# Two-layer AdaLN/MoE kernel: the second layer's input and token rows turned by transposing DMAs instead of identity matmuls

## What is computed

```python
# layer 0: per-sequence mixed weight, then a top-2 mixture of 8 linear experts
h = einsum('bnt,bot->bno', x, einsum('bg,got->bot', cond, weight * mask)) + bias
probs = softmax(h @ router_w.T); top-2 of 8
x = x + sum over the two experts of (h @ expert_w + prob) * topk_weight
# layer 1: per-sequence projection with LoRA, then shared and routed SwiGLU
h = einsum('btc,oc->bto', x, W_base) + b_base + 2 * lora(x, As, Bs, cond)
shared = sum over 2 experts of silu(h @ wg) * (h @ wu) @ wd        # width 352 each
probs = softmax(h @ gate_w); top-2 of 8, weights normalized
routed = sum over the two experts of w * swiglu_e(h)
x = x + shared + routed
```

## Time and profile before

| | |
|---|---|
| median of 3 runs | 382.75 us (382.38 to 382.76) |
| the profiled execution | 382.96 us, its span 380.9 us |
| PE busy | 362.4 us, 95% of the span |
| DVE, ACT, POOL busy | 63%, 44%, 41% |
| granted TensorE clock, mean | 0.993 of full speed |

### The profile page before, as it was taken

How to read it: one execution, slowest core, us unless ns; L and a number is a source line. 1 busy time by engine, 2 the same in 40 slices (tenths; PEclk the granted TensorE clock), 3 DMA queues, 4 the chain that set the end, 5 groups by cost and what they waited for, 6 DMA issues and landing times.

```text
span 380.9 us, 7891 instructions
## 1 busy us (share of the span) xinstructions
PE 362.4 (95%) x2671; PEld 222.6 (58%) x2672; DVE 238.6 (63%) x594; ACT 166.6 (44%) x286; POOL 155.8 (41%) x241
## 2 busy tenths in 40 slices
PE   7998999999999999889999899999999999999992
PEld 2354444454454555455446677777777777766570
DVE  1367999776657547787774455565556556546574
ACT  1145377467655675451441333333333333322560
POOL 3000564656537631000020365565565556422652
PEclk9999999999999999999999999999999999999997
DMA  7975213433353410100000122222222222213922
GB/s 232 391 289 202 75 41 108 147 114 113 129 179 98 141 55 2 56 2 0 2 28 2 42 85 83 69 83 81 71 81 83 82 70 83 69 43 138 353 90 109
DMA packets 18037, 39.24 MB, mean 103 GB/s; under 512 B 2976, under 2 KB 9376, under 8 KB 17888
## 3 DMA queue, kind: packets, MB, share of 16 engines
q1 hardware_dynamic: 13552, 28.71, 22.2%
q0 software_dynamic: 3744, 10.23, 8.5%
q10 hardware_dynamic: 720, 0.02, 0.1%
HBM read 29.65 MB, written 9.31 MB: 102 GB/s over the span
## 4 chain that ended last, share of the span: by engine, by line
PE 73%; DVE 16%; issue 3%; ACT 3%; DMA 2%; POOL 1%; POOLq 0%; ACTq 0%; SPq 0%; DVEq 0%
PE bank L998 57%; PE bank L1145 7%; PE bank L1243 3%; DVE prod L903 2%; DVE x L776 2%; PE bank L1227 2%; PE bank L1014 2%; ACT acts L581 2%; DMA x<-wc 2%; DVE x L891 1%; DVE w0s L646 1%; DVE acts L908 1%; DVE hs L634 1%; ACT sil L571 1%; PE bank L1074 1%
## 5 line engine op out<-in xcount | busy, mean ns | idle before, releaser
L442 POOL TENSOR_TENSOR w1s<-piece,w1s 128x170 f16<-128x170 f32 x128 | 61.6, 520 | 78.5 <-ACT piece L531 78.5
L998 PE MATMUL bank<-w0s,hs 128*128 128x512 f16 x384 | 86.2, 379 | 1.4 <-DVE x L776 1.2
L998 PE MATMUL bank<-w1s,rT 128*128 x468 | 76.2, 313 | 1.5 <-DVE rT L962 1.5
L451 POOL DMA_INDIRECT rows<-token_store,row_in x39 | 38.0, 974 | 88.2 <-DVE row_in L873 48.5
L776 DVE SCALAR_TENSOR_TENSOR x<-bank,coef,x 128x256 f32<-128x256 f32 x128 | 54.8, 478 | 19.3 <-PE bank L998 19.0
L998 PEld LDWEIGHTS bank<-w0s,hs 128*128 128x128 f16 x384 | 36.9, 98 | 44.1 <-DVE x L776 1.9
L998 PE MATMUL bank<-hs,w1s 128*128 128x512 f16 x264 | 59.3, 379 | 1.9 <-DVE prod L903 1.9
L998 PEld LDWEIGHTS bank<-w1s,rT 128*128 128x128 f16 x468 | 44.0, 98 | 22.0 <-issue 2.0
L456 POOL DMA_INDIRECT results<-yb,row_out x39 | 38.6, 990 | 37.0 <-ACT yb L605 37.0
L998 PE MATMUL bank<-w1s,aT 128*128 (+1 forms) x351 | 44.8, 272 | 0.8 <-DVE aT L955 0.8
L599 ACT ACTIVATE ract<-prod 128x352 f16<-128x352 f32 x39 | 19.4, 498 | 58.4 <-DVE prod L968 33.6
(11 more groups left out here) (149 smaller groups left out, 405.4 us busy)
## 6 DMA issues: line engine op xcount, KB each, us to landing
piece<-w SPq DMA_DIRECT2D x16, 680.0 KB, 3.9
w1s<-results SPq DMA_DIRECT2D x6, 512.0 KB, 9.4
x<-wc SPq DMA_DIRECT2D x4, 512.0 KB, 6.7
w1s<-xT SPq DMA_DIRECT2D x4, 512.0 KB, 10.2
w1s<-w SPq DMA_DIRECT2D x4, 512.0 KB, 8.8
token_store<-xrow SPq DMA_DIRECT2D x4, 512.0 KB, 2.9
out<-x SPq DMA_DIRECT2D x8, 256.0 KB, 2.0
x<-x SPq DMA_DIRECT2D x1, 1536.0 KB, 10.6
```

Of the source, the lines that this page charges most:

```text
L442: ins = nc.gpsimd.tensor_tensor(w1s[:, LO, at], piece[:, i % 2, part], w1s[:, HI, at], ALU.subtract)
L451: pool.indirect_dma_start(rows[:, i % 2], None, token_store, bass.IndirectOffsetOnAxis(row_in[:, i:i + 1], 0)).then_inc(s_row[i % 2], 16)
L998: mm = nc.tensor.matmul(out_ap, l, r, start=(i == 0), stop=(i == len(terms) - 1))
```

## The change

The input of layer 1 is split into halves first, in the layout in which `x1` lies (`xh`, a new buffer of 256 KB for one pair of tiles), and then turned by one transposing DMA for each pair from SP, `turn_input(m)`. The token rows of a chunk are turned by four transposing DMAs, `turn_rows(c)`, from `hs` into `xrow`. PE's `transposes` and `token_rows`, and ACT's `copy_rows`, are gone. `tr_hi(m)` waits for the combines of its pair and, as `xh` is a single buffer, for the turn before. `tr_lo(m-1)` stands behind j=0 instead of j=2. On SP, turn_input stands behind pieces 3, 5, ... 15 and at the end, turn_rows behind pieces 8 and 12, keep behind pieces 9 and 13 (waiting for the transfers of turn_rows to land), and at the end come turn_rows(2), keep(2), turn_input(7), turn_rows(3), keep(3). layer1_input(3) and all of the routing move one step of gate_up later, down(0) too.

```diff
-    DOWN = {ST + 1: 0, EARLY - 1: 1, EARLY + 1: 2}
+    DOWN = {ST + 2: 0, EARLY - 1: 1, EARLY + 1: 2}
...
+        xh = sb("xh", [P, 2, 2, D], F16)
...
+            def turn_input(m):
+                sp.wait_ge(sm["s_trlo"], m + 1)
+                sp.dma_start_transpose(xrow[:, 2 * m:2 * m + 2].rearrange("p t (b n) -> p (t b) n", n=P),
+                                       xh[:].rearrange("p t a w -> p (t a w)")).then_inc(sm["s_xt"], 16)
+
+            def turn_rows(c):
+                sp.wait_ge(sm["s_hlo"], (B + c + 1) * KT)
+                for a in range(2):
+                    for k in range(KT):
+                        o = (a * KT + k) * P
+                        sp.dma_start_transpose(xrow[:, c * TPB:(c + 1) * TPB, o:o + P],
+                                               hs[:, a, k, c * S:(c + 1) * S]).then_inc(sm["s_rows"], 16)
+
             def keep(c):
-                sp.wait_ge(sm["s_rows"], (c + 1) * TPB)
+                sp.wait_ge(sm["s_rows"], 16 * 2 * KT * (c + 1))
...
                 sp.dma_start(piece[:, i % 2], w1_flat[:, i * PIECE:(i + 1) * PIECE]).then_inc(s_piece[i], 16)
+                if i >= 3 and i % 2 == 1:
+                    turn_input(i // 2 - 1)
                 if i in (8, 12):
+                    turn_rows(i // 4 - 2)
+                if i in (9, 13):
                     keep(i // 4 - 2)
 
+            turn_rows(2)
             keep(2)
+            turn_input(TWO - 1)
+            turn_rows(3)
             keep(3)
...
             def tr_hi(m):
-                act.wait_ge(sm["s_tr"], m + 1)
-                nc.scalar.activation(xs[:, 2 * m:2 * m + 2, HI], turned(), ACT.Copy, scale=SX).then_inc(sm["s_trhi"], 1)
+                act.wait_ge(sm["s_comb"], (m + 1) * 2 * E)
+                if m == 0:
+                    act.wait_ge(sm["s_bias"], 2)
+                else:
+                    act.wait_ge(sm["s_xt"], 16 * m)
+                nc.scalar.activation(xh[:, :, HI], x1[:, 2 * m:2 * m + 2], ACT.Copy, scale=SX).then_inc(sm["s_trhi"], 1)
...
-                if m >= 3 and m % 2 == 1:
-                    copy_rows((m - 3) // 2)
...
-                if i == 1:
+                if i == 2:
                     h_hi(1, B - 1)
...
-                    if j == 2 and m >= 1:
+                    if j == 0 and m >= 1:
                         tr_lo(m - 1)
...
-                if i == 2:
+                if i == 3:
                     take_logits(1, 0, ALL)
...
-                if i == 14:
+                if i == 15:
                     tile_experts()
...
             def layer1_input(c):
 
-                pe.wait_ge(sm["s_trlo"], (c + 1) * TPB // 2)
+                pe.wait_ge(sm["s_xt"], 16 * (c + 1) * TPB // 2)
                 pe.wait_ge(sm["s_wllo"], c + 1)
-                if c >= 1:
-                    pe.wait_ge(sm["s_rows"], c * TPB)
...
-                    if j == 1 and m >= 1:
-                        transposes(m - 1)
...
-                gate_up(i, TWO - 1 if i == 0 else None)
-                if i == 1:
+                gate_up(i)
+                if i == 2:
                     layer1_input(B - 1)
-                if i == 2:
+                if i == 3:
                     logits(1, B - 1)
-                if i == 3:
-                    token_rows(B - 1, (0, 1))
-                if i == 4:
-                    token_rows(B - 1, (2, 3))
+                if i == 5:
                     ranks()
```

More of the change, by code:

```diff
@@ L233, in build_program @@
             "s_wllo",
-            "s_tr",
+            "s_xt",
             "s_trhi",
@@ L735, in tr_lo @@
                 dve.wait_ge(sm["s_trhi"], m + 1)
-                nc.vector.scalar_tensor_tensor(xs[:, 2 * m:2 * m + 2, LO], turned(), SX, xs[:, 2 * m:2 * m + 2, HI],
+                nc.vector.scalar_tensor_tensor(xh[:, :, LO], x1[:, 2 * m:2 * m + 2], SX, xh[:, :, HI],
                                                ALU.mult, ALU.subtract).then_inc(sm["s_trlo"], 1)
@@ L932, in _ @@
                     nc.vector.tensor_copy(sel16[:, NT:], t1[:]).then_inc(sm["s_sel"], 1)
-                if i == 4:
+                if i == 5:
                     groups()
-                if i == 5:
+                if i == 6:
                     slots()
-                if 8 <= i < 11:
-                    hot_tiles(i - 8)
-                if i == 12:
+                if 9 <= i < 12:
+                    hot_tiles(i - 9)
+                if i == 13:
                     slot_tokens()
-                if i == 14:
+                if i == 15:
                     tile_experts()
@@ L1120, in _ @@
                             layer1_input(c)
-                        if j == 2:
-                            pe.wait_ge(sm["s_hlo"], (B + c + 1) * KT)
-                            token_rows(c, (0, 1))
                         if j == 3:
@@ L1127, in _ @@
                             logits(1, c)
-                            token_rows(c, (2, 3))
             def down(c, parts=(range(ST),)):
@@ L1136, in down @@
                             if c == 0:
-                                pe.wait_ge(sm["s_rows"], NT)
                                 pe.wait_ge(sm["s_slots"], 1)
@@ L1149, in down, with gate_up @@
                             mm.then_inc(sm["s_dn"], 1)
-            def gate_up(i, between=None):
+            def gate_up(i):
                 c, f, p = i // ST, i % ST, side(i)
@@ L1160, in gate_up @@
                 for g in range(2 if f < ST - 1 else 1):
-                    if g and between is not None:
-                        transposes(between)
                     mm = group(bank[2 * p + g][0:P if f < ST - 1 else 2 * REST],
```

2 lines of the change are left out of this document (removed).

## The result

The changed kernel takes 395.44 us (median of 4 runs, 391.65 to 396.26) against 382.75: ratio 1.028, 95% interval 1.024 to 1.032, 12.7 us slower. The profiled execution took 396.26 us, its span is 394.5. The page: busy time of PE, its slices, the granted clock in slices, the chain by engine.

What follows compares the result with a forecast made beforehand. PE, busy 95% of the span, was taken as the bound; the 7.1 us taken off it were used up by waits on ACT and DVE. 382.75 + 0.5 (order) + 5.5 (transfers) = 388.8 us, range 381.0 to 422.

Steps and rivals of the forecast that it cites:

- sign: Whole kernel: the change was forecast to make it slower, with chance 0.70 for slower, 0.18 same, 0.12 faster.
- (a): Layer 0, m=1: DVE waits 1.5 us for tr_hi(0), everything behind is 2.1 us later, PE waits about 1 us.
- (b): Layer 0, m=2: DVE waits for tr_hi(1), PE's combine comes 3.1 us later, layer 1's first product at about 76.4 us.
- (c): Layer 0, m=3 to 7: PE waits 0.4 us three times on odd m, leaving layer 0 0.5 us earlier than before.
- (d): Routing moved later: PE waits 2.7 us for sel instead of 0.69; down(0) starts at 166.5 instead of 165.05 us.
- (e): From down(0) to the routed loop: table wait about 2 us instead of 0.36, stretch 42.4 to 43.0 us instead of 43.6.
- transfers' term: Transposing transfers: 2.5 us per 256 KB, 1.25 per 128 KB, 1 to 1.5 us per SP issue; about +5.5 us.
- packet price of 9.6 ns: Upper bound for transposing transfers, from queue q10's 28 B packets: 4.9 us for 256 KB in 32 B pieces.
- first rival: Transfers are cheap, 1 us or less for 256 KB, issues near 0.4 us: +0.3 to +0.7, 383.3 us; chance 0.27.
- faster rival: Layer 0: ACT reaches split(2m) early, tr_hi is ready for DVE, waits shrink from 3.1 to 1 us; 380.5 us; chance 0.12.

Runs made afterwards that it cites:

- act_first: The changed kernel with tr_hi(m-1) ahead of split_piece(2m) on ACT instead of behind it; 384.38 us.
- fill_waits: The changed kernel with PE's three long waits in the routing part filled by matmuls on zeros whose results are not used; 391.57 us.
- late_routing: The kernel before with only layer1_input(3), the routing and down(0) one gate_up step later, identity matmuls kept; 390.83 us, ratio 1.017.
- rows_only: The kernel before with only the token rows turned by transposing transfers, layer 1's input still on PE; 380.16 us, ratio 0.993.
- lo_late: The changed kernel with tr_lo(m-1) on DVE back behind j=2, all else as changed; 391.61 us.

## Why the prediction was right in sign, and where its steps failed

**Steps (a) and (b) held.** PE's waits at m=1 and 2 (1.06, 1.42, 0.55, 2.17 us) brought layer 1's first product 3.2 us later, once the start is taken off; 3.1 were forecast. DVE stood 3.00 us before tr_lo(1), as ACT's `tr_hi` came at 71.20. act_first shows that ACT's order is the cause of the long ones; the 1.06 us stays there too.

**Step (c): right mechanism, too small.** PE waited 0.97 us three times instead of 0.4. The step that failed is "`tr_hi`/`tr_lo` keep their size and read SBUF": tr_lo took 1.05 us in the median, against 0.68 from PSUM, and stands in the chain that frees the banks. That the 0.4 us more in tr_lo is what made 0.4 into 0.97 is worked out, not tested. The waits are 1.7 of the 2.6 us missing in this stretch; most of the rest is the 0.16 us of pipeline that nothing overlaps behind a wait, three times, and small gaps (60 matmuls in 13.24 and 13.43 us, where they take 13.11 in act_first).

**Step (d) held.** `sel` was waited for 2.87 us (2.7 forecast), and from chunk 3's product to down(0) it was 23.8 us; without the drop, in act_first and fill_waits, it is 22.6, against 22.2.

**Step (e) was under-priced.** "In small waits -0.5 to +0.1" is wrong: gate_up(12) waited 2.0 us instead of 0.89, because the one-hot work of DVE moved with the routing, and the table was waited for 2.8 to 2.9 instead of 2 us. Without a drop in the clock the stretch is 44.8 us (162.67 to 207.47 in act_first) instead of the 42.4 to 43.0 forecast, 1.8 to 2.4 us more. late_routing shows that this half needs no transfer to cost 5 us or more.

**The transfers' term failed.** 5.5 us were forecast from 2.5 us for 256 KB; the rings need 1.2, and what reached PE was 0.63 us at turn 7, 0.9 with what surrounds it; plain copies took 2.5 us off the median, which is the most that the form of the transfers can account for. My packet price of 9.6 ns for some 28 B had nothing to do with these transfers: they move in packets of about 256 B (under 512 B there are 17152 more of them than before, for 4.2 MB). The issue time was right. Of the first rival's condition the size nearly held (1.2 us of the rings against 1), the issue did not (1.24 us against 0.4). Its 383.3 us did not come out either, since (c) and (e) lacked 4 to 5 us and the clock was left out.

The Trainium skill's 261 GB/s (DMA: Bandwidth & Descriptors, Latency and other measured facts) was the better guide here: 214 GB/s measured. Its 1309 ns for a 128x128 block (VectorE: DVE Perf Modes, The three transpose paths) did not add up block by block: a transfer of eight blocks took 1.2 us of the rings, not 10.5.

**The granted clock was missing from the sum.** Nothing in it priced what a wait of PE does to the matmuls behind it. Here that was some 6.1 of 12.6 us in the profiled run, 2.7 of them behind waits that the change made or lengthened; fill_waits shows these. The 3.4 at the start, behind waits of 2.01 and 1.62 us, are no part of the change's mechanism: nothing up to there is edited. late_routing, which up to there is the kernel before, has the second of them too, and rows_only waited 2.37 us at the first place without a drop. So it is partly chance what a run loses by it.

Without the clock the change cost some 6.5 us to the loop's start, against 6.0 forecast, but that agreement is luck: transfers too dear by 4.6 us or so went against (c) and (e) too cheap by 4 to 5. The sign was right, and the other half of the 12.7 us was the term that the sum didn't have.

**The faster rival's mechanism was real, but not in this kernel.** DVE's waits behind ACT decide over layer 0, as it says; ACT had to be reordered for it, which the change didn't do.

## What to carry to other kernels

When work is taken off a full engine, ask who stands next in each queue that the replacement passes: here a product on DVE placed two steps early waited for ACT, PE waited for DVE, and the 7.1 us were gone with transfers that hardly cost anything. Moving the helper on the third engine (ACT) ahead of the long work that doesn't need to be first brought the kernel back to about where it had been (384.38 against 382.6 us). Only with the routing back in its place too was it faster than before, by 3 us. The token rows alone had already given 2.4 us, and the two kernels (378.94 and 379.83 against 380.16 us) were not run beside each other; so how much the turning of the input adds is not shown.

Don't shift a long serial chain (routing) later to cover a transfer until the transfer's landing has been measured; the cover cost 5 us, the wait that it covered was 0.23 to 0.49 us once the transfer stood first in SP's queue.

Price a wait of PE of 1.6 us and more at its length plus, in some executions, 1.7 us of slow matmuls behind it (2.9 once). In others the same wait costs only its length.

## What the runs showed of the hardware

Two engines slowed each other where an all-SBUF product on DVE met POOL. In the kernel after, eight subtractions on POOL take 3.78 us, but 4.23 where a tr_lo runs beside them (the second row; tr_lo at 86.55 took 1.05 us):

```profile
80.12 3.78 POOL L463 TENSOR_TENSOR w1s<-piece,w1s 128x170 f16<-128x170 f32 x8 [3.29 <-ACT piece L550]
86.07 4.23 POOL L463 TENSOR_TENSOR w1s<-piece,w1s 128x170 f16<-128x170 f32 x8 [2.17 <-ACT piece L550]
```

With POOL idle the same tr_lo took 0.68 us, as from PSUM (lo_late, at 59.60 us). The row below, from act_first, took 0.68 us too, though POOL was at work: there a subtraction of POOL began 0.02 us behind it, and took 1.04 us instead of 0.51.

```profile
88.34 0.68 DVE L749 SCALAR_TENSOR_TENSOR xh<-x,xh 128x512 f16<-128x512 f32 x1
```

The Trainium skill (SBUF — State Buffer, Who interferes with whom) says that a DVE instruction with two SBUF inputs contends with a GpSimd instruction that reads SBUF, and that the later one waits; the traces agree, 0.37 us on DVE and 0.45 on POOL in the kernel after, and nothing on DVE where it came first.

Four transposing transfers of 128 KB issued one after another keep SP for 5.1 to 6.2 us. Where they run alone (the last four, 5.13 us) the rings need 2.4 us for them, about half: there the issue, not the bandwidth, is the limit (1.27 us each).
